# Moving copies and two tables from VectorE to ScalarE, and re-ordering TensorE's fillers, in a two-layer decoder kernel

## The chip, the cores and the metric

The kernel runs on one core of a Trainium2 chip. A core has TensorE (PE in the profile; PEld is its weight load), VectorE (DVE), ScalarE (ACT), GpSimd (POOL) and SyncE (SP), which issues the DMAs. Each engine runs its own list of instructions in order, and they wait for each other by semaphores. The metric is the device time of one execution in microseconds (us).

## The reference

The input `x` is (2, 512, 128), with a context (2, 154, 128). Six blocks are added to `x` one after the other: an attention with a window (A), a top-32 cross attention (B), an FP4-quantised feed-forward (C), a six-layer linear-attention encoder (D), a cross attention (E), and a six-layer block (F), which is more than half of the time and the place of nearly all of the change. F computes:

```python
for i in range(DEPTH):                       # DEPTH = 6
    x = attn_layer(shift_tokens(x), Wqkv[i], q_scale[i], k_scale[i], Wo[i]) + x
    x = ffn_layer(shift_tokens(x), ln_g[i], ln_b[i], W1[i], b1[i], W2[i], b2[i]) + x
# shift_tokens: the second half of the 128 channels moves by one position
# attn_layer:  qkv = x @ Wqkv, 16 heads of 64; q = l2norm(q) * qs; k = l2norm(k) * ksc
#              rotary position with a scale per channel, window 32 (each block sees itself and the one before),
#              softmax(8 * q k^T) v, then @ Wo
# ffn_layer:   xn = layernorm(x) * g + b; a, gate = split(xn @ W1 + b1)  (341 columns each)
#              (a * gelu(gate)) @ W2 + b2
```

## The kernel before

Activations stay in SBUF for the whole kernel, channels on the 128 partitions and 512 positions of a batch along the free dimension. PSUM is one tensor `ps` with eight banks of 128x512; `take` makes PE wait until the last reader of a bank is done, `read` is what that reader says. Most tiles are parts of one buffer, `big` or `fix`, so the profile's names say little and its line numbers more.

F has twelve **units**, numbered 0 to 11 here: layer 0 with batch 0, layer 0 with batch 1, layer 1 with batch 0, and so on. A unit is the attention of its layer and batch. The feed-forward of unit n runs as **hooks** inside the attention of unit n+1 (which has the other batch), so that the two chains fill each other's waits. All orders are written out by hand, one function for each engine. One unit has three parts.

- **Head**: `a_proj_pe`, with what `a_tail_pe` of the unit before has already done (pairs 0 to 2). Heads are handled as eight pairs p = 0..7. For each pair PE makes Q and K (L285, L290) in banks p % 2 and 2 + p % 2, ACT squares them (L487, L489), DVE multiplies them with the rotary tables (`a_rope_dve`, L607, L608), SP swaps neighbouring partitions by DMA (L738), and POOL adds (L705, L706). PE sums the squares (`a_ss_pe`, L331, bank 5), ACT makes the reciprocal roots in three steps (L513, L515, L516, signal `n_ready`), and PE spreads them over the partitions (`a_spread_q_pe`, `a_spread_k_pe`; L339 for pair 0, L341 for the others, from a three-part bf16 copy made by ACT and DVE). V has eight products of 512 columns (`a_v_pe`, L274), copied by ACT (L479). In the head stand the hooks of the feed-forward before: centre (L2015), variance (L2030), three pairs of products gate and up (L2038, L2040; ACT's Gelu L2105, DVE's product L2159), and `f_down_pe` (L2046), three products that end in bank Y = 7.
- **Steps** p = 0..7 (`a_steps_pe`): the mask is written into banks 0 and 1 (L372, or L367 at p = 7), which waits for DVE's last read of them; `a_scores_pe` (L384) adds the scores; DVE (`a_top_dve`) takes the maximum (L656 twice) and subtracts it (L659 twice), then multiplies Q of the next pair with its spread (L621), then sums the exponentials (L642, L649); ACT takes the exponential (L542); POOL normalises (L714, two halves). PE transposes the probabilities of step p-1 (`a_turn_pe`, L398), ACT copies them (L554), PE multiplies those of step p-2 with V (`a_values_pe`, L415), ACT copies the result (L547), PE adds pair p-3 to the output (`a_out_pe`, L425). DVE has late hooks: after step 1 it adds the feed-forward of the unit before to `x` (`f_add_dve`, L2164), after step 3 it copies `x` shifted into `xsh` for the next unit (`shift_dve`, L2133, L2134), and after step 5 of every odd unit but the last it scales the rotary tables for the next layer (`f_tab_dve`, L2171, four products). Below, "top of step p" is the group L656, L659.
- **Tail** (`a_tail_pe`): what is left of steps 6 and 7 on PE, with Q and K of pairs 0 to 2 of the next unit between.

The attention A uses the same functions without the spreads and without the feed-forward.

## Time and profile before

| | |
|---|---|
| median of 3 runs | 1751.95 us (1751.57 to 1753.41) |
| the profiled execution | 1752.89 us |
| its span, first to last instruction | 1751.1 us |
| PE busy | 1573.1 us, 90% |
| DVE, ACT, POOL busy | 1183.6, 904.8, 593.2 us (68%, 52%, 34%) |
| mean granted clock of PE | 0.961 |

Busy shares are means over blocks with different limits. A row of the timeline is a run of equal instructions: its start, its length, the line, and in brackets how long the engine had been idle before, with what ended that. The ends of matmuls are modelled, so for products back to back the distance between starts is the better measure: in F a product of 128x512 f32 (two passes) starts 0.86 us after the one before.

### The profile page before, as it was taken

The numbers are of one execution on the slowest core, as the hardware profiler recorded it, in microseconds if no ns is written. First come the engines' busy times: TensorE is split into PE (matmuls) and PEld (weight loads), VectorE is DVE, ScalarE is ACT, GpSimd is POOL, SyncE is SP. The second block draws the span as 40 slices with busy tenths as digits, with TensorE's granted clock in tenths as the row PEclk, the third lists the DMA queues.
The fourth block names the chain that finished last, engine by engine and source line by source line (L and its number), as shares of the span: only waits on it lengthen the run. The fifth ranks groups of instructions, "written<-read, shape, count | busy, mean of one in ns | idle before, by whom it ended". The sixth has DMA issues, their size and how long they took to land.

```text
span 1751.1 us, 37919 instructions
## 1 busy us (share of the span) xinstructions
PE 1573.1 (90%) x15445; PEld 855.6 (49%) x15445; DVE 1183.6 (68%) x2048; ACT 904.8 (52%) x1584; POOL 593.2 (34%) x552
## 2 busy tenths in 40 slices
PE   7887569999999998779999999999999999999996
PEld 2645336565566554223645445363545545353543
DVE  5686576656566654347778778677877867787773
ACT  2435334344533443335665656666566666666663
POOL 5362000000000000105564655445465655555561
PEclk9899779999999999879999999999999999999998
DMA  7134100000000000203041322314142231314120
GB/s 248 28 118 193 54 0 7 2 21 1 21 21 1 21 1 1 93 1 122 30 145 60 96 99 70 129 33 135 56 125 82 86 125 31 127 65 131 68 64 13
DMA packets 50668, 119.41 MB, mean 68 GB/s; under 512 B 15297, under 2 KB 20161, under 8 KB 48321
## 3 DMA queue, kind: packets, MB, share of 16 engines
q1 hardware_dynamic: 50496, 116.99, 20.3%
q8 instruction: 125, 2.05, 0.5%
q14 instruction: 47, 0.38, 0.1%
HBM read 37.52 MB, written 0.52 MB: 22 GB/s over the span
## 4 chain that ended last, share of the span: by engine, by line
PE 52%; DVE 28%; ACT 9%; issue 5%; DMA 3%; POOL 2%; SPq 1%; DVEq 0%; ACTq 0%
DVE nm L656 4%; PE ps L1583 3%; DVE nm L642 3%; PE ps L285 3%; PE ps L425 3%; PE ps L415 3%; PE ps L290 3%; PE ps L1636 3%; PE ps L274 3%; DVE big L659 2%; PE ps L1645 2%; DMA big<-big 2%; DVE big L607 2%; PE ps L1602 2%; DVE big L608 2%
## 5 line engine op out<-in xcount | busy, mean ns | idle before, releaser
L714 POOL TENSOR_TENSOR big<-big,nm 128x384 f32<-128x384 f32 x224 | 189.7, 867 | 186.5 <-DVE nm L649 186.5
L705 POOL TENSOR_TENSOR big<-big 128x512 f32<-128x512 f32 x112 | 143.3, 1280 | 310.8 <-DMA big<-big 309.8
L607 DVE TENSOR_TENSOR big<-ps,big 128x512 f32<-128x512 f32 x224 | 153.7, 686 | 87.3 <-ACT sq L487 55.8
L542 ACT ACTIVATE big<-big 128x384 f32<-128x384 f32 x224 | 109.4, 522 | 126.7 <-DVE big L659 126.6
L1427 POOL MEMSET big<- 128x512 f32 x1 | 0.5, 526 | 489.0 <-DVE x L1910 489.0
L608 DVE TENSOR_TENSOR big<-ps,big 128x512 f32<-128x512 f32 x224 | 152.5, 681 | 0.0
L415 PE MATMUL ps<-big 128*64 128x64 f32 x3584 | 130.6, 226 | 23.1 <-ACT big L554 22.9
L415 PEld LDWEIGHTS ps<-big 128*64 128x64 f32 x3584 | 116.5, 139 | 63.5 <-ACT big L554 46.6
L706 POOL TENSOR_TENSOR big<-big 128x512 f32<-128x512 f32 x112 | 144.5, 1290 | 0.0
L1870 DVE TENSOR_TENSOR big<-ps,fix 128x512 f32<-128x512 f32 x192 | 119.2, 683 | 37.3 <-PE ps L1583 36.9
L398 PE MATMUL ps<-ident,big 128*128 128x128 f32 x896 | 129.3, 283 | 15.2 <-POOL big L714 13.2
L698 POOL TENSOR_TENSOR big<-big 128x512 f32<-128x512 f32 x84 | 107.2, 1276 | 71.7 <-ACT big L534 71.6
L656 DVE TENSOR_REDUCE nm<-ps 128x4 f32<-128x384 f32 x224 | 112.3, 543 | 26.9 <-PE ps L384 24.3
L554 ACT ACTIVATE big<-ps 128x512 f32<-128x512 f32 x224 | 122.3, 594 | 9.8 <-PE ps L398 8.0
L479 ACT ACTIVATE big<-ps 128x512 f32<-128x512 f32 x112 | 66.7, 595 | 112.8 <-PE ps L274 112.8
L398 PEld LDWEIGHTS ps<-ident,big 128*128 128x128 f32 x896 | 97.8, 142 | 40.5 <-POOL big L714 27.3
L659 DVE TENSOR_TENSOR big<-ps,nm 128x384 f32<-128x384 f32 x224 | 113.5, 549 | 0.3
L642 DVE TENSOR_REDUCE nm<-big 128x8 f32<-128x768 f32 x96 | 91.5, 953 | 21.8 <-ACT big L542 20.0
L274 PE MATMUL ps<-big,xsh 128*128 128x512 f32 x192 | 104.7, 628 | 0.0
L384 PE MATMUL ps<-big 64*64 64x96 f32 (+1 forms) x3584 | 97.3, 244 | 5.5 <-DVE big L627 2.2
L285 PE MATMUL ps<-xsh,big 128*128 128x512 f32 x192 | 100.6, 606 | 0.2 <-DVE big L608 0.2
L425 PE MATMUL ps<-fix,big 128*128 128x512 f32 x192 | 99.6, 600 | 0.7 <-ACT fix L547 0.7
(301 smaller groups left out, 2930.9 us busy)
## 6 DMA issues: line engine op xcount, KB each, us to landing
big<-big SPq DMA_DIRECT2D x224, 256.0 KB, 2.4
big<-big SPq DMA_DIRECT2D x112, 128.0 KB, 2.4
big<-in_F_w SPq DMA_DIRECT2D x6, 1536.0 KB, 7.0
big<-in_zero SPq DMA_DIRECT2D x8, 1088.0 KB, 12.5
big<-big SPq DMA_DIRECT2D x84, 64.0 KB, 2.0
big<-in_D_w SPq DMA_DIRECT2D x12, 256.0 KB, 3.0
big<-in_F_wo SPq DMA_DIRECT2D x6, 512.0 KB, 4.3
big<-in_F_w SPq DMA_DIRECT2D x6, 341.0 KB, 3.0
```

The lines of the kernel that those rows point to most:

```text
L274: pe.matmul(ps[:, kv, :], src_of(key, b)[:, 128 * t:128 * t + 128], Wqkv[:, 2, 512 * hf:512 * hf + 512], start=True, stop=True).then_inc(* ...
L285: pe.matmul(ps[:, kq, :], Wqkv[:, 0, 128 * p:128 * p + 128], src_of(key, b), start=True, stop=True).then_inc(*full[kq].mark((key, b, "q", p)))
L398: last = pe.transpose(ps[:, 4 + h, 128 * j:128 * j + 128], P[:, 2 * (p % 2) + h, at0:at0 + 128], ident[:, :])
L415: last = pe.matmul(ps[64 * h:64 * h + 64, 6, 64 * m:64 * m + 64], vv[:, m // 2, 128 * p + 64 * h:128 * p + 64 * h + 64], PT[:, 2 * (p % 2) ...
L425: last = pe.matmul(ps[:, Y, :], Wo[:, p, :], ot(key, p), start=p == 0, stop=p == NP - 1)
L607: dve.tensor_tensor(tmp[:, i, w, :], ps[:, k, :], tb[:, 2 * w, :], ALU.mult).then_inc(*part.mark((key, b, p, 0)))
L608: dve.tensor_tensor(sinp[:, i, T * w:T * w + T], ps[:, k, :], tb[:, 2 * w + 1, :], ALU.mult).then_inc(*part.mark((key, b, p, 1)))
L642: dve.tensor_reduce(nm[:, i, 8:16].rearrange("p (h j) -> p h j", h=2), P[:, g:g + 2, :].rearrange("p h (j k) -> p h j k", j=4)[:, :, :, 0: ...
L656: dve.tensor_reduce(nm[:, i, 4 * h:4 * h + 4], s4(h), AX, ALU.max).then_inc(*topped.mark((key, b, p, h)))
L659: dve.tensor_tensor(shft[:, 2 * (p % 2) + h, :].rearrange("p (j k) -> p j k", j=4), s4(h), nm[:, i, 4 * h:4 * h + 4].unsqueeze(2).to_broad ...
L706: pool.tensor_tensor(KT[:, p, :], tmp[:, i, 1, :], swp[:, i, T:2 * T], ALU.add).then_inc(*k_added.mark((key, b, p)))
L714: pool.tensor_tensor(v, v, nm[:, p % 3, 16 + 4 * h:20 + 4 * h].unsqueeze(2).to_broadcast([128, 4, KW]), ALU.mult)\
```

## The change

Five things are changed.

1. The shifted copy of `x` into `xsh` for the next unit and the scaling of the rotary tables go from DVE to ACT: `f_move_act` after step 3, `f_tab_act` in two halves after steps 4 and 5 of odd units. The tables of layer 0 are still made by DVE.
2. DVE adds the feed-forward to `x` before step 0 instead of after step 1. `f_down_pe` is cut: its first two products stand behind the spreads of pair 0, its third behind the scores of step 0.
3. The third `up` product of the feed-forward goes to bank 2 instead of bank 7.
4. On PE, V 5 stands before the spreads of pair 0, and in steps 1 to 6 the spreads stand between the mask and the scores instead of behind the scores.
5. In the tail, Q 0 of the next unit stands before the values of step 6 and K 0 behind them; Q 1 and K 1 stand before the output product of pair 6.

The transposes of the probabilities stay as they are.

```diff
@@ a_qk_pe is split @@
-        def a_qk_pe(pe, key, b, p):
-            kq, kk = p % 2, 2 + p % 2
+        def a_q_pe(pe, key, b, p):
...
+        def a_k_pe(pe, key, b, p):
...
+        def a_qk_pe(pe, key, b, p):
+            a_q_pe(pe, key, b, p)
+            a_k_pe(pe, key, b, p)
@@ a_proj_pe @@
                 a_ss_pe(pe, key, b, NP // 2 - 1)
-                a_v_pe(pe, key, b, 4)
+            a_v_pe(pe, key, b, 4)
+            a_v_pe(pe, key, b, 5)
+            if l2:
+                a_spread_q_pe(pe, key, b, 0)
+                a_spread_k_pe(pe, key, b, 0)
                 if "down" in hooks:
                     hooks["down"]()
-                a_spread_q_pe(pe, key, b, 0)
-                a_spread_k_pe(pe, key, b, 0)
-            else:
-                a_v_pe(pe, key, b, 4)
-            a_v_pe(pe, key, b, 5)
@@ a_steps_pe @@
                 a_mask_pe(pe, key, b, p, l2)
+                if l2 and p >= 2 and p + 2 < NP:
+                    a_spread_k_pe(pe, key, b, p + 2)
+                if l2 and 0 < p < NP - 1:
+                    a_spread_q_pe(pe, key, b, p + 1)
                 a_scores_pe(pe, key, b, p, l2)
-                if l2 and p + 1 < NP:
-                    a_spread_q_pe(pe, key, b, p + 1)
                 if l2 and p == 0:
+                    a_spread_q_pe(pe, key, b, 1)
                     a_spread_k_pe(pe, key, b, 1)
+                if p in late:
+                    late[p]()
                 if p < 2:
                     a_v_pe(pe, key, b, NT + 2 + p)
-                if l2 and p + 2 < NP:
-                    a_spread_k_pe(pe, key, b, p + 2)
-                if p in late:
-                    late[p]()
+                    if l2:
+                        a_spread_k_pe(pe, key, b, p + 2)
@@ a_tail_pe @@
+            if nxt:
+                a_q_pe(pe, *nxt, 0)
             a_values_pe(pe, key, b, NP - 2)
+            if nxt:
+                a_k_pe(pe, *nxt, 0)
             a_out_pe(pe, key, b, NP - 3)
-            if nxt:
-                a_qk_pe(pe, *nxt, 0)
             a_turn_pe(pe, key, b, NP - 1)
-            a_out_pe(pe, key, b, NP - 2)
             if nxt:
                 a_qk_pe(pe, *nxt, 1)
...
+            a_out_pe(pe, key, b, NP - 2)
             a_values_pe(pe, key, b, NP - 1)
@@ a_rope_dve, attn_dve @@
+            if l2 and n == -3 and key[1] > 0:
+                dve.wait_ge(*tab_made.at((key[1], 1)))
...
                     a_parts_dve(dve, key, b)
+                if "down" in early:
+                    early["down"]()
@@ f_up_pe, f_down_pe, f_pe_hooks @@
+        UP = (7, 7, 2)
...
-            take(pe, 7)
-            pe.matmul(ps[0:m, 7, :], W1[:, c0:c0 + m], fxn, start=True, stop=True).then_inc(*full[7].mark(("F", l, b, "up", i)))
+            take(pe, UP[i])
+            pe.matmul(ps[0:m, UP[i], :], W1[:, c0:c0 + m], fxn, start=True, stop=True).then_inc(*full[UP[i]].mark(("F", l, b, "up", i)))
...
-                     "up": lambda: f_up_pe(pe, *u, 2), "down": lambda: f_down_pe(pe, *u)}, {})
+                     "up": lambda: f_up_pe(pe, *u, 2), "down": lambda: f_down_pe(pe, *u, (0, 1))}, {0: lambda: f_down_pe(pe, *u, (2,))})
@@ new functions of ACT, and their hooks @@
+        def f_move_act(act, l, b):
+            act.wait_ge(*x_new.at(("Ff", l, b)))
+            step(act, act_step, act.activation(xsh[0:64, b, :], x[0:64, cols(b)], ACT.Copy))
+            act.activation(xsh[64:128, b, 1:T], x[64:128, T * b:T * b + T - 1], ACT.Copy).then_inc(moved, 1)
+
+        def f_tab_act(act, l, i):
+            act.wait_ge(scl_in, 16 * (l + 1))
+            act.wait_ge(*k_part.at((("F", l - 1), B - 1, NP - 1, 1)))
+            for j in (2 * i, 2 * i + 1):
+                ins = act.activation(tab[:, j, :], tab0[:, j, :], ACT.Copy, scale=scl[:, i:i + 1])
+            ins.then_inc(*tab_made.mark((l, i)))
...
+            l, late = key[1], {3: lambda: f_move_act(act, *u)}
+            if b == B - 1 and l + 1 < LAYERS:
+                late[4], late[5] = lambda: f_tab_act(act, l + 1, 0), lambda: f_tab_act(act, l + 1, 1)
@@ f_dve_hooks @@
-            def move():
-                dve.wait_ge(*x_new.at(("Ff", *u)))
-                shift_dve(dve, u[1], (moved, 1))
...
-                early = {4: lambda: f_scale_dve(dve, *u), 6: lambda: f_mul_dve(dve, *u, 0), 7: multiply}
-                late[1], late[3] = lambda: f_add_dve(dve, *u), move
+                early = {4: lambda: f_scale_dve(dve, *u), 6: lambda: f_mul_dve(dve, *u, 0), 7: multiply,
+                         "down": lambda: f_add_dve(dve, *u)}
...
-            if b == B - 1 and l + 1 < LAYERS:
-                late[5] = lambda: f_tab_dve(dve, l + 1)
```

How the order moves. On PE, from the last sum of squares in the head to the spread of K of pair 2, in unit 1, before (L331 sum of squares, L274 V, L2046 down, L339 and L341 spreads, L372 mask, L384 scores):

```order
L331 MATMUL ps<-big 32x512 x4
L274 MATMUL ps<-big,xsh 128x512
L2046 MATMUL ps<-fix,big 128x512 x3
L339 MATMUL ps<-rs,big 128x512 x2
L274 MATMUL ps<-big,xsh 128x512
L372 MATMUL ps<-band,identb 64x384 x4
L384 MATMUL ps<-big 64x64 x2
L384 MATMUL ps<-big 64x96 x14
L341 MATMUL ps<-xn,big 128x512 x2
L274 MATMUL ps<-big,xsh 128x512
L341 MATMUL ps<-xn,big 128x512
```

And in the changed kernel, where the same are L336, L274, L2064, L344, L346, L377 and L389:

```order
L336 MATMUL ps<-big 32x512 x4
L274 MATMUL ps<-big,xsh 128x512 x2
L344 MATMUL ps<-rs,big 128x512 x2
L2064 MATMUL ps<-fix,big 128x512 x2
L377 MATMUL ps<-band,identb 64x384 x4
L389 MATMUL ps<-big 64x64 x2
L389 MATMUL ps<-big 64x96 x14
L346 MATMUL ps<-xn,big 128x512 x2
L2064 MATMUL ps<-fix,big 128x512
L274 MATMUL ps<-big,xsh 128x512
L346 MATMUL ps<-xn,big 128x512
```

V 5 has moved ahead of the spreads, and one of the three down products now stands behind the scores of step 0.

On DVE, from the last of the three parts to the add of the feed-forward, in the same unit, before (L636 last part of the three, L656 and L659 top, L621 Q, L642 and L649 sum, L2164 the add):

```order
L636 SCALAR_TENSOR_TENSOR xn<-xn,eps,sq 128x512
L656 TENSOR_REDUCE nm<-ps 128x4 x2
L659 TENSOR_TENSOR big<-ps,nm 128x384 x2
L621 TENSOR_TENSOR big<-big,ps 128x512
L642 TENSOR_REDUCE nm<-big 128x8
L649 RECIPROCAL nm<-nm 128x8
L656 TENSOR_REDUCE nm<-ps 128x4 x2
L659 TENSOR_TENSOR big<-ps,nm 128x384 x2
L621 TENSOR_TENSOR big<-big,ps 128x512
L642 TENSOR_REDUCE nm<-big 128x8
L649 RECIPROCAL nm<-nm 128x8
L2164 SCALAR_TENSOR_TENSOR x<-ps,big,x 128x512
```

And changed (L648, L668, L671, L633, L654, L661, and L2199 for the add):

```order
L648 SCALAR_TENSOR_TENSOR xn<-xn,eps,sq 128x512
L2199 SCALAR_TENSOR_TENSOR x<-ps,big,x 128x512
L668 TENSOR_REDUCE nm<-ps 128x4 x2
L671 TENSOR_TENSOR big<-ps,nm 128x384 x2
L633 TENSOR_TENSOR big<-big,ps 128x512
L654 TENSOR_REDUCE nm<-big 128x8
L661 RECIPROCAL nm<-nm 128x8
L668 TENSOR_REDUCE nm<-ps 128x4 x2
```

The add now stands ahead of the top of step 0.

On PE, the end of step 7 and the tail of unit 1, before (L415 values, L398 transposes, L425 output, L285 and L290 Q and K of the next unit):

```order
L415 MATMUL ps<-big 64x64 x16
L398 MATMUL ps<-ident,big 128x128 x8
L425 MATMUL ps<-fix,big 128x512
L415 MATMUL ps<-big 64x64 x16
L425 MATMUL ps<-fix,big 128x512
L285 MATMUL ps<-xsh,big 128x512
L290 MATMUL ps<-xsh,big 128x512
L398 MATMUL ps<-ident,big 128x128 x8
L425 MATMUL ps<-fix,big 128x512
```

And changed (L420, L403, L430, L284, L292):

```order
L420 MATMUL ps<-big 64x64 x16
L403 MATMUL ps<-ident,big 128x128 x8
L430 MATMUL ps<-fix,big 128x512
L284 MATMUL ps<-xsh,big 128x512
L420 MATMUL ps<-big 64x64 x16
L292 MATMUL ps<-xsh,big 128x512
L430 MATMUL ps<-fix,big 128x512
L403 MATMUL ps<-ident,big 128x128 x8
L284 MATMUL ps<-xsh,big 128x512
```

One Q product now stands ahead of the values of step 6, and its K product behind them.

## Rows read from the trace of the kernel before

**Rows 1.** Waits of PE in F: us in total, times, longest.

```profile
PE ps L415 <- ACT big L554: 18.3, 39, 1.1
PE ps L372 <- DVE big L659: 9.8, 22, 0.5
PE ps L2040 <- DVEq L136: 6.1, 6, 1.4
```

**Rows 2.** Instructions of L689: ns min/median/max, first and last start in us.

```profile
L689 DVE TENSOR_TENSOR x<-x,ps x14: 686/689/689, 90.2 to 1723.8; 128x512 f32<-128x512 f32 x14
```

**Rows 3.** Timeline, PE, unit 7, V 4 to step 1: start us, us, instruction.

```profile
1364.40 1.13 PE L274 MATMUL ps<-big,xsh 128*128 128x512 f32 x2
1365.36 2.74 PE L2046 MATMUL ps<-fix,big 128*128 128x512 f32 x6
1368.03 1.13 PE L339 MATMUL ps<-rs,big 32*128 32x512 f32 x4
...
1370.70 0.89 PE L384 MATMUL ps<-big 64*64 64x64 f32 x32 [0.20 <-DVE big L627]
...
1371.84 1.13 PE L274 MATMUL ps<-big,xsh 128*128 128x512 f32 x2
...
1373.72 0.36 PE L372 MATMUL ps<-band,identb 64*64 64x384 bf16 x4 [0.43 <-DVE big L659]
```

**Rows 4.** Timeline, ACT, unit 7, the reciprocal roots.

```profile
1364.73 0.69 ACT L513 ACTIVATE rs<-ps,eps 128x512 f32<-128x512 f32 x1
...
1366.29 0.72 ACT L516 ACTIVATE rs<-rs,eps 128x512 f32<-128x512 f32 x1
1367.04 0.63 ACT L518 ACTIVATE xn<-rs 128x512 bf16<-128x512 f32 x1
```

**Rows 5.** Timeline, DVE, unit 7, steps 0 to 2.

```profile
1371.62 1.02 DVE L656 TENSOR_REDUCE nm<-ps 128x4 f32<-128x384 f32 x2 [0.41 <-PE ps L384]
...
1375.17 0.95 DVE L642 TENSOR_REDUCE nm<-big 128x8 f32<-128x768 f32 x1 [1.01 <-ACT big L542]
...
1379.87 0.70 DVE L2164 SCALAR_TENSOR_TENSOR x<-ps,big,x 128x512 f32<-128x512 f32 x1
```

**Rows 6.** Timeline, PE, unit 6, head to tail.

```profile
1286.12 1.09 PE L2040 MATMUL ps<-xc,big 128*85 128x512 f32 x2 [0.98 <-DVEq L136]
...
1301.06 1.44 PE L398 MATMUL ps<-ident,big 128*128 128x128 f32 x8 [0.52 <-POOL big L714]
...
1304.79 1.31 PE L398 MATMUL ps<-ident,big 128*128 128x128 f32 x8
1306.56 0.36 PE L372 MATMUL ps<-band,identb 64*64 64x384 bf16 x4 [0.46 <-DVE big L659]
...
1317.27 1.15 PE L415 MATMUL ps<-big 128*64 128x64 f32 x32 [0.20 <-ACT big L554]
...
1324.37 0.49 PE L367 MATMUL ps<-bandw,identb 128*128 128x384 bf16 x2
...
1329.78 1.15 PE L415 MATMUL ps<-big 128*64 128x64 f32 x32 [1.14 <-ACT big L554]
```

**Rows 7.** Timeline, PE, unit 5 (with tables), steps 7 and tail.

```profile
1246.59 0.48 PE L367 MATMUL ps<-bandw,identb 128*128 128x384 bf16 x2 [0.82 <-DVE big L659]
...
1248.56 1.15 PE L415 MATMUL ps<-big 128*64 128x64 f32 x32 [0.58 <-ACT big L554]
...
1252.31 1.15 PE L415 MATMUL ps<-big 128*64 128x64 f32 x32 [0.67 <-ACT big L554]
```

**Rows 8.** Waits of ACT in F: us in total, times, longest.

```profile
ACT big L542 <- DVE big L659: 94.6, 66, 4.0
```

**Rows 9.** Windows: PE, PEld, DVE, ACT, POOL busy (instructions), PE clock, DMA, GB/s.

```profile
820.00:824.00 4.00, 1.44 (x6) 0.30 (x2) 3.54 (x6) 3.27 (x6) 0.81 (x2) 1.00 0.48 161
824.00:832.00 8.00, 7.89 (x47) 2.96 (x47) 6.99 (x9) 2.00 (x4) 6.99 (x5) 0.57 0.50 141
1246.00:1250.00 4.00, 2.82 (x69) 2.23 (x70) 3.82 (x8) 2.69 (x6) 1.55 (x2) 1.00 0.01 4
```

More of the change, by code:

```diff
@@ L281, in a_qk_pe @@
             if p < 2:
-                take(pe, kq)
+                take(pe, p)
             else:
                 pe.wait_ge(*q_part.at((key, b, p - 2, 1)))
-            pe.matmul(ps[:, kq, :], Wqkv[:, 0, 128 * p:128 * p + 128], src_of(key, b), start=True, stop=True).then_inc(*full[kq].mark((key, b, "q", p)))
+            pe.matmul(ps[:, p % 2, :], Wqkv[:, 0, 128 * p:128 * p + 128], src_of(key, b), start=True, stop=True).then_inc(*full[p % 2].mark((key, b, "q", p)))
+        def a_k_pe(pe, key, b, p):
+            kk = 2 + p % 2
             if p < 2:
@@ L1998, in build @@
         f_const, scl_in, ff_in_ = raw("f_const"), raw("scl_in"), raw("ff_in_")
-        tab_made = sg("tab_made")
+        tab_made, tab_first = sg("tab_made"), sg("tab_first")
         F_FF = 5 * 16
@@ L2038, in f_up_pe, with f_down_pe @@
             pe.matmul(ps[0:m, 6, :], W1[:, DI + c0:DI + c0 + m], fxn, start=True, stop=True).then_inc(*full[6].mark(("F", l, b, "gate", i)))
-            take(pe, 7)
-            pe.matmul(ps[0:m, 7, :], W1[:, c0:c0 + m], fxn, start=True, stop=True).then_inc(*full[7].mark(("F", l, b, "up", i)))
-        def f_down_pe(pe, l, b):
-            take(pe, Y)
-            for i, (c0, m) in enumerate(DIC):
+            take(pe, UP[i])
+            pe.matmul(ps[0:m, UP[i], :], W1[:, c0:c0 + m], fxn, start=True, stop=True).then_inc(*full[UP[i]].mark(("F", l, b, "up", i)))
+        def f_down_pe(pe, l, b, parts):
+            for i in parts:
+                if i == 0:
+                    take(pe, Y)
+                m = DIC[i][1]
                 pe.wait_ge(*f_mul.at((l, b, i)))
                 last = pe.matmul(ps[:, Y, :], W2[0:m, i, :], fh[0:m, i, :], start=i == 0, stop=i == 2)
-            last.then_inc(*full[Y].mark(("F", l, b, "f2")))
+            if i == 2:
+                last.then_inc(*full[Y].mark(("F", l, b, "f2")))
         def f_before(l, b):
@@ L2070, in f_pe @@
                 f_up_pe(pe, *u, i)
-            f_down_pe(pe, *u)
+            f_down_pe(pe, *u, range(3))
         def f_square_act(act, l, b):
@@ L2119, in f_act_hooks @@
             return ({3: lambda: f_square_act(act, *u), 4: lambda: f_root_act(act, *u), 5: lambda: f_xn_act(act, *u), 6: lambda: f_gelu_act(act, *u, 0),
-                     7: lambda: f_gelu_act(act, *u, 1), "up": last}, {})
+                     7: lambda: f_gelu_act(act, *u, 1), "up": last}, late)
         def f_act(act):
@@ L2156, in f_mul_dve @@
             m = DIC[i][1]
-            dve.wait_ge(*full[7].at(("F", l, b, "up", i)))
+            dve.wait_ge(*full[UP[i]].at(("F", l, b, "up", i)))
             dve.wait_ge(*gg.at((l, b, i)))
-            dve.scalar_tensor_tensor(fh[0:m, i, :], ps[0:m, 7, :], b1[0:m, i:i + 1], fg[i % 2][0:m, :], ALU.add, ALU.mult).then_inc(*f_mul.mark((l, b, i)))
-            read(dve, 7, f_mul, (l, b, i))
+            dve.scalar_tensor_tensor(fh[0:m, i, :], ps[0:m, UP[i], :], b1[0:m, i:i + 1], fg[i % 2][0:m, :], ALU.add, ALU.mult).then_inc(*f_mul.mark((l, b, i)))
+            read(dve, UP[i], f_mul, (l, b, i))
         def f_add_dve(dve, l, b):
@@ L2171, in f_tab_dve @@
                 ins = dve.tensor_scalar(tab[:, j, :], tab0[:, j, :], scl[:, j // 2:j // 2 + 1], None, ALU.mult)
-            ins.then_inc(*tab_made.mark(l))
-            dve.wait_ge(*tab_made.at(l))
+            ins.then_inc(*tab_first.mark(l))
+            dve.wait_ge(*tab_first.at(l))
         def f_dve_hooks(dve, key, b):
@@ L2247, in f_sp @@
                 if l + 1 < LAYERS:
-                    sp.wait_ge(*tab_made.at(l))
+                    sp.wait_ge(*(tab_made.at((l, 1)) if l else tab_first.at(0)))
                     f_w_sp(sp, l + 1)
```

## The prediction

> **What bounds the kernel now.** I read the busy shares first, then who waits for whom on PE in F, then the timelines of PE, DVE and ACT over two units. F's units follow each other in 77.2 us: the last add of a unit first starts at 875.0 us in F and last at 1723.8, eleven units on [rows 2]. PE sets that length. Over the 27 us of a head it has at most one gap above 0.3 us, and its four steps 3 to 6 take 17.8 us (1306.56 to 1324.37 [rows 6]), nearly all of it work. What it loses stands in short waits that come back at the same places in every unit: for ACT's copies of the transposes ahead of the values (18.3 us in 39 waits), for DVE's subtraction ahead of the mask (9.8 us), and for bank 7 ahead of the third `up` product (6.1 us in six heads, those of unit 5 and the even units from 2 on) [rows 1]. So the question is what each new order does to these waits. DVE is next: where a hook stands in its steps it, and not PE, sets the pace.
>
> **Head to step 0.** Take unit 7, whose head has no wait for bank 7. V 4 starts at 1364.40 [rows 3], 0.86 us of work. V 5 now comes next, but it needs bank 5, which L513 reads until 1365.42 [rows 4]: it starts at 1365.5, not at 1365.3, and takes PE to 1366.5. The spreads of pair 0 wait for `n_ready`, which is L516's end, 1367.01 [rows 4]; so PE idles 0.6 us where it had none, and the spreads start at 1367.1 instead of 1368.03 [rows 3]. They take 1.06. Two down products (0.86 each, from 2.74 for three: 2 x 0.86 + 1.02 [rows 3]) end at about 1369.95, and the scores follow 0.36 after the mask, at 1370.3 instead of 1370.70: **-0.4**. In even units the wait of 0.98 for bank 7 goes too [rows 6], since bank 2 was last read by the rotary products of pair 6, long done. There L513 had waited for the sums of squares behind it; it moves forward until it meets the end of the table load, so nearly all of it is kept: **-1.0** more.
>
> **Step 0.** This is where the change costs. DVE's add now stands ahead of the top of step 0, and the add waits for the third down product. From the scores' start: scores and spreads 1.14 (1370.70 to 1371.84), product 1.02, 0.1 to hand over [rows 3], so the add starts at 1370.3 + 2.26 = 1372.55. An add of this form holds DVE 0.8 (0.70 and its signal [rows 5]). The top of step 0 starts at 1373.35 and not at 1371.62 [rows 5], and the mask of step 1, which waits for that top, moves from 1373.72 [rows 3] by the same: **+1.75** in odd units, **+0.75** in even ones. PE has nothing for the time: behind the product it has V 6 and one spread, as before.
>
> **Steps 1 to 3.** Some of it comes back. (a) The sum of step 0 waited 1.01 us for ACT's exponential [rows 5], which ACT took up late behind V 6 and the spread's copy; these now come before the top is done. The sum starts 0.95 earlier against the mask, and so do POOL and the transposes, ahead of which PE waited 0.52 and which took 1.44 where those a step later took 1.31 and nothing but POOL's second half held them [rows 6]: **-0.8**. (b) The add no longer stands in DVE's way after step 1 (1379.87 [rows 5]): that was the mask's wait of 0.46 before step 3 and, with it, slower scores and values in step 3 [rows 6]. Of some 0.9 in all I take **-0.65**, the rest staying as a wait.
>
> **Steps 3 to 6.** DVE's copies (1.35 us) go: the wait of 0.20 ahead of values at step 5 [rows 6] goes with them, **-0.2**. PE works without gaps there, so no more can come. The spreads in front of the scores delay scores by 0.3 and so top, exponential and copies; the values of step p need the copies of the transposes of p-2, which by the trace were ready about as much ahead of them. I take 0, bounded by -0.2 and by +0.3 in each of six steps (+1.8 a unit). In odd units with tables the four DVE products go, which made PE wait 0.82 before the mask of step 7 and 0.58 behind it, against 0.67 instead of 1.14 in the tail [rows 6, 7]: 0.82 + 0.58 - 0.47 = **-0.93** in five units.
>
> **What ACT takes over.** Two copies per unit, four table copies in five units. The trace has no ACT copy of 64 rows; the nearest are 0.63 us (the bf16 copy of the reciprocal roots) and 0.72 with an operand per partition [rows 4], so 0.63 to 0.72 each, 1.3 for a pair. ACT waits for DVE's subtraction 94.6 us over F in 66 waits, 1.4 on average [rows 8]. Behind `f_move_act` stands the spread's copy and then the exponential of the next step, which waits for just that subtraction: the pair fits with 0.1 us to spare. So 0, bounded above by the pair in full, 1.3 x 11 moves + 2.6 x 5 tables = 27 us. ACT's only wait that could be new is for `scl`; its DMA is issued in step 1 and lands some 6.5 us later, before step 4.
>
> **The tail.** Values of step 6 wait 1.14 us for ACT's copies in plain units and 0.67 after tables [rows 6, 7]. Q 0 (0.86) now fills that: the values start where they did, and all that follows is one product shorter: **-0.86**. Q 0 needs bank 0, free when the top of step 7 is done, 1.2 us before, and `xsh`, copied by ACT three steps earlier. ACT's squares can begin earlier, so the rotary part gets a start; PE had no wait there, so 0. Q 1 and K 1 before the output of pair 6 swap work that both was ready: 0.
>
> **The sum.** Odd units with tables: +1.75 - 0.8 - 0.65 - 0.2 - 0.93 - 0.86 = -1.7. Even units: +0.75 - 0.8 - 0.65 - 0.2 - 0.86 = -1.75. Five of each: -17.25. Unit 5 has a wait for bank 7 too, 0.65: -0.65. Unit 0 has no feed-forward and gets the tail only: -0.86. Unit 11 has neither tables nor a next unit: +1.75 - 0.8 - 0.65 - 0.2 = +0.1. In A the waits of the tail are elsewhere: 0. Total -18.7. The profiled execution took 1752.89 us (span 1751.1); that gives 1734.2, and on the median of 1751.95 it gives **1733 us**, 1.1% less.
>
> **Rivals.**
> *A, the late product costs nothing.* If the top of step 0 is not delayed, or if steps 1 to 3 give all of it back, +1.75 and +0.75 fall away: 6 x 1.75 + 5 x 0.75 = 14, so 1719. For it: DVE has 4 us a unit less to do in the steps than before. Against: PE, not DVE, sets steps 3 to 6, so DVE's slack buys nothing there, and DVE is in order.
> *B, ACT's new work comes onto the path.* The copies of the transposes stand behind it, and PE already waits for these more than for anything [rows 1]. If half of the 27 us shows, the time is 1747; that is still faster, just so.
> *C, the clock falls in each unit, and the kernel is slower.* [...] The order of now never brings this on in units 1 to 10: even 1246 to 1250, with PE idle 1.2 of 4 us, stayed at 1.00 [rows 9]. The new order gathers 0.6 us ahead of the spreads and, from there 5 us on, a wait ahead of the mask of step 1: PE reaches it at 1373.7 and the mask comes at 1375.45, 1.7 us, more than any wait F has now outside units 0 and 11. [...]
> [...]
>
> **How the numbers follow.** My forecast 0.64, A 0.16, B 0.12, C 0.08. A measurement of this kernel tells a difference of about 0.2%, 3.5 us. The forecast's own range is 1724 to 1741, from the ends of the ACT and scores terms. A pulls to 1715 and B to 1747: 1713 to 1747 leaves out most of C and little else. Faster: 0.62 + 0.16 + 0.10 = 0.88; within 0.2%: 0.05; slower: 0.07.
>
> **What would show it.** In the new profile of a middle unit: (1) no wait at the third `up`; (2) a wait of 0.5 to 0.7 us ahead of the spreads of pair 0; (3) the add directly behind the third down product, and a wait of 1.2 to 1.8 us ahead of the mask of step 1, the largest of the unit; (4) values of step 6 with a wait of 0.3 or less and Q 0 in front; (5) steps 3 to 6 in some 17 us instead of 17.8, with waits ahead of the values below 0.2; (6) clock 1.00 in units 1 to 10; (7) a unit of 75.5 us instead of 77.2. Waits of 0.5 and more for L564 (ACT's copies) would speak for B; a granted clock below 1 in the middle of F, for C; no wait at (3), for A. I am wrong if steps 3 to 6 take less than 16.5 us, since then PE was not what set them.

## The result, and the profile after

| | before | changed |
|---|---|---|
| median, timed on the same chip | 1752.68 us | 1780.79 us (1778.61 to 1785.29) |
| ratio, 95% interval | | 1.0165 (1.0148 to 1.0183) |
| profiled execution, span | 1752.89, 1751.1 us | 1778.61, 1776.8 us |
| PE busy | 1573.1 us | 1605.6 us |
| mean granted clock | 0.961 | 0.948 |

It is 1.6% slower; the forecast was 1733, in 1713 to 1747. In the changed kernel L377 and L372 are the mask, L389 the scores, L344 (pair 0) and L346 the spreads, L420 the values, L403 the transposes, L430 the output, L284 and L292 Q and K, L2064 down, L2056 `up`, L2029 the centre. Engine rows of its page (busy us, share, instructions):

```profile
PE 1605.6 (90%) x15445; PEld 863.2 (49%) x15445; DVE 1182.4 (67%) x2006; ACT 927.4 (52%) x1626; POOL 590.0 (33%) x552
```

PE executes the same 15445 instructions, and yet is busy 32.5 us longer: it ran more of them slowly. Then who PE waits for in F (line, releaser: us in total, times, longest):

```profile
PE ps L377 <- DVE big L671: 20.4, 11, 1.9
PE ps L2056 <- DVEq L136: 7.5, 7, 1.7
PE ps L420 <- ACT big L564: 6.0, 22, 1.0
PE ps L344 <- ACT rs L526: 4.6, 11, 0.4
PE ps L2029 <- DVE xsh L2169: 2.1, 10, 0.3
```

Against [rows 1] the waits for ACT's copies fell from 18.3 to 6.0 us, those for DVE's subtraction rose from 9.8 to 20.4 and lie in one place, and a wait for `xsh` is new. The wait for bank 7 is gone from the third `up`, but it has come back at the second, and is longer there: 7.5 us in seven heads, where it was 6.1 in six. The timeline of PE in unit 7, which answers to [rows 3]:

```profile
1382.91 2.24 PE L274 MATMUL ps<-big,xsh 128*128 128x512 f32 x4
1385.58 1.13 PE L344 MATMUL ps<-rs,big 32*128 32x512 f32 x4 [0.42 <-ACT rs L526]
...
1388.55 0.36 PE L377 MATMUL ps<-band,identb 64*64 64x384 bf16 x4
...
1393.97 0.36 PE L377 MATMUL ps<-band,identb 64*64 64x384 bf16 x4 [1.85 <-DVE big L671]
...
1395.61 1.13 PE L274 MATMUL ps<-big,xsh 128*128 128x512 f32 x2
...
1396.98 1.20 PE L403 MATMUL ps<-ident,big 128*128 128x128 f32 x8
...
1400.04 1.15 PE L420 MATMUL ps<-big 128*64 128x64 f32 x32 [0.42 <-ACT big L564]
```

The mask waits 1.85 us, for DVE's subtraction, which stands behind the add (DVE in unit 7: the add, the maximum, the subtraction):

```profile
1390.98 0.75 DVE L2199 SCALAR_TENSOR_TENSOR x<-ps,big,x 128x512 f32<-128x512 f32 x1 [1.95 <-PE ps L2064]
1391.87 1.02 DVE L668 TENSOR_REDUCE nm<-ps 128x4 f32<-128x384 f32 x2
1392.81 1.01 DVE L671 TENSOR_TENSOR big<-ps,nm 128x384 f32<-128x384 f32 x2
```

The same stretch of unit 6 begins alike and goes on otherwise:

```profile
1313.42 0.36 PE L377 MATMUL ps<-band,identb 64*64 64x384 bf16 x4 [1.85 <-DVE big L671]
...
1315.05 2.08 PE L274 MATMUL ps<-big,xsh 128*128 128x512 f32 x2
...
1317.59 1.97 PE L403 MATMUL ps<-ident,big 128*128 128x128 f32 x8
...
1320.49 1.53 PE L389 MATMUL ps<-big 64*64 64x64 f32 x32
```

The same products take 2.08 instead of 1.13 us, and 1.97 instead of 1.20. The windows of the two stretches (unit 6, then unit 7; columns as in [rows 9]) say why:

```profile
1308.00:1321.00 13.00, 11.00 (x112) 5.50 (x115) 8.59 (x16) 6.17 (x12) 5.76 (x6) 0.77 0.31 76
1389.00:1402.00 13.00, 10.45 (x158) 5.84 (x149) 9.98 (x21) 6.68 (x13) 7.15 (x8) 1.00 0.41 113
```

The granted clock was 0.77 in the first, a mix of 1.00 up to 1315.0 and 0.50 from there on, and 1.00 in the second. A fall of the clock stands behind the wait in nine of the eleven units (not in 1 and 7); in units 2, 3, 5, 6 and 10 the granted clock over steps 0 to 3 is 0.84, in 4, 8, 9 and 11 it is 0.91. Over the span, 1776.8 x (1 - 0.948) = 92 us of full-speed work are lost, against 1751.1 x (1 - 0.961) = 68 before.

Where the time went, from the starts of the masks in units 1 to 10 (sums in us; the forecast is my terms put into the same parts, good to some 0.5 each):

| part of a unit | before | changed | difference | forecast |
|---|---|---|---|---|
| step 0 | 35.7 | 55.0 | +19.3 | +19.0 |
| steps 1 to 3 | 140.4 | 146.5 | +6.2 | -14.5 |
| steps 4 to 6 | 133.7 | 130.8 | -2.9 | -6.1 |
| mask of step 7 to the next unit's first | 466.9 | 467.3 | +0.4 | -16.3 |
| sum | 776.7 | 799.6 | +22.9 | -17.9 |

Another 3.3 us lie ahead of unit 1, 2.8 of them in unit 0 (79.15 instead of 76.34). So three parts are off, and the one that I called the cost is not among them.

### The profile page after: what moved, and what is told of

The parts are those of the page before. It is cut to its first block, busy times and chain, and to the rows that moved or that the text cites. A ratio compares the mean times of both kernels' runs of the same rounds, so it can differ in the third digit from the quotient of the medians.

```text
span 1776.8 us, 37924 instructions
## 1 busy us (share of the span) xinstructions
PE 1605.6 (90%) x15445; PEld 863.2 (49%) x15445; DVE 1182.4 (67%) x2006; ACT 927.4 (52%) x1626; POOL 590.0 (33%) x552
## 4 chain that ended last, share of the span: by engine, by line
PE 60%; DVE 19%; ACT 11%; issue 4%; DMA 2%; POOL 2%; SPq 0%; DVEq 0%; ACTq 0%; POOLq 0%
PE ps L420 5%; PE ps L403 5%; PE ps L430 5%; PE ps L389 4%; PE ps L1597 3%; PE ps L292 3%; PE ps L1650 3%; DVE big L619 3%; DVE big L620 3%; DVE nm L668 2%; PE ps L1659 2%; DMA big<-big 2%; PE ps L274 2%; PE ps L284 2%; PE ps L1616 2%
## 5 line engine op out<-in xcount | busy, mean ns | idle before, releaser
L728 POOL TENSOR_TENSOR big<-big,nm 128x384 f32<-128x384 f32 x224 | 185.0, 847 | 182.4 <-DVE nm L661 182.4
L668 DVE TENSOR_REDUCE nm<-ps 128x4 f32<-128x384 f32 x224 | 114.2, 551 | 52.0 <-PE ps L389 48.1
L403 PE MATMUL ps<-ident,big 128*128 128x128 f32 x896 | 131.5, 291 | 8.3 <-POOL big L728 7.3
L420 PE MATMUL ps<-big 128*64 128x64 f32 x3584 | 129.2, 225 | 10.6 <-ACT big L564 10.1
L420 PEld LDWEIGHTS ps<-big 128*64 128x64 f32 x3584 | 115.1, 138 | 44.4 <-ACT big L564 26.7
L403 PEld LDWEIGHTS ps<-ident,big 128*128 128x128 f32 x896 | 102.8, 147 | 31.2 <-POOL big L728 13.3
L671 DVE TENSOR_TENSOR big<-ps,nm 128x384 f32<-128x384 f32 x224 | 113.2, 546 | 0.0
L274 PE MATMUL ps<-big,xsh 128*128 128x512 f32 x192 | 110.3, 660 | 0.0
L654 DVE TENSOR_REDUCE nm<-big 128x8 f32<-128x768 f32 x96 | 91.5, 953 | 26.9 <-ACT big L552 25.2
L389 PE MATMUL ps<-big 64*64 64x96 f32 (+1 forms) x3584 | 102.9, 252 | 1.5 <-DVE big L639 1.5
L284 PE MATMUL ps<-xsh,big 128*128 128x512 f32 x192 | 101.7, 611 | 2.1 <-DVE big L620 2.1
L292 PE MATMUL ps<-xsh,big 128*128 128x512 f32 x192 | 100.5, 605 | 0.8
```

Source lines behind the costliest of these rows:

```text
L274: pe.matmul(ps[:, kv, :], src_of(key, b)[:, 128 * t:128 * t + 128], Wqkv[:, 2, 512 * hf:512 * hf + 512], start=True, stop=True).then_inc(* ...
L284: pe.matmul(ps[:, p % 2, :], Wqkv[:, 0, 128 * p:128 * p + 128], src_of(key, b), start=True, stop=True).then_inc(*full[p % 2].mark((key, b, ...
L292: pe.matmul(ps[:, kk, :], Wqkv[:, 1, 128 * p:128 * p + 128], src_of(key, b), start=True, stop=True).then_inc(*full[kk].mark((key, b, "k", p)))
L389: last = pe.matmul(ps[64 * c_:64 * c_ + 64, h, KW * j + k0:KW * j + KW], Q[rows, p, 64 * m:64 * m + 64], KT[rows, p, 64 * m - WIN + k0:64 ...
L403: last = pe.transpose(ps[:, 4 + h, 128 * j:128 * j + 128], P[:, 2 * (p % 2) + h, at0:at0 + 128], ident[:, :])
L420: last = pe.matmul(ps[64 * h:64 * h + 64, 6, 64 * m:64 * m + 64], vv[:, m // 2, 128 * p + 64 * h:128 * p + 64 * h + 64], PT[:, 2 * (p % 2) ...
```

## The experiments

In step lengths below, a step is the time from one mask to the next. All kernels compute the whole reference. They were timed on three chips; each ratio is to the kernel before on the same chip, whose medians there are 1752.6 to 1753.8. Where two runs come from different chips, a difference of their medians is good to a few us.

### The late add, and the clock behind its wait

`x1_add_late` is the changed kernel with DVE's add behind step 1 again:

```diff
-                early = {4: ..., 6: ..., 7: multiply, "down": lambda: f_add_dve(dve, *u)}
+                early = {4: ..., 6: ..., 7: multiply}
+                late[1] = lambda: f_add_dve(dve, *u)
```

> The changed kernel with one edit: DVE adds the feed-forward to x after step 1 again, as before the change; the three down products stay where the change put them. Theory 1 (the add ahead of the top of step 0 makes the mask of step 1 wait 1.85 us, and that wait brings the clock down in 9 of 11 units): the interval from the mask of step 0 to that of step 1 goes from 5.42 to about 3.7 us, no fall of the granted clock in the middle of F; 11 x 1.7 for the wait and 9 x 2.2 for the clock, less some 0.5 a unit that the add costs at its old place: about 1748 us. Theory 2 (it is the spreads between mask and scores, 0.16 us in every step): the time stays within 5 us of the changed kernel's 1781. Theory 3 (the heads lose it, since the new tail makes the shifted copy meet POOL's adds): also within 5 us of 1781.

Measured: 1760.91 us, ratio to before 1.0041 (1.0025 to 1.0058); 20 us come back. Step 0 takes 3.50 instead of 5.42, but step 1 takes 5.48 instead of 4.14: PE waits before the transposes.

```profile
1381.29 1.44 PE L403 MATMUL ps<-ident,big 128*128 128x128 f32 x8 [1.24 <-POOL big L728]
```

Its cause is on ACT, which in this unit had DVE's subtraction (done by 1376.7) to work on, but stood at V 6, whose product came later; the exponential follows the second of these rows, at 1378.2:

```profile
1376.97 0.60 ACT L489 ACTIVATE big<-ps 128x512 f32<-128x512 f32 x1 [1.29 <-PE ps L274]
1377.69 0.60 ACT L544 ACTIVATE big<-ps 128x512 f32<-128x512 f32 x1
```

So step (a) of the forecast was real, but it was bought by the early add: without that, V 6 and the spread's copy stand in the exponential's way as before, and V 6 comes later still, since the third down product now stands ahead of it (step 1 takes 5.48 where it took 4.98 before the change). The clock still fell in five units, here behind the wait of 1.24. With that wait and those falls the time is 13 us above the 1748 that theory 1 gave.

`x2_fill` leaves the order of the changed kernel and puts two products that nobody reads into PE's wait before the mask of step 1 (into bank 4, which is free there):

```diff
+                    if l2 and p == 0 and (key, b) != F_UNITS[0]:
+                        pe.wait_ge(*v_ready.at((key, b, 4)))
+                        for _ in range(2):
+                            pe.matmul(ps[:, 4, :], src_of(key, b)[:, 0:128], Wqkv[:, 2, 0:512], start=True, stop=True)
```

> The changed kernel with two extra products of 128x512 f32 into bank 4, which nobody reads, in PE's wait ahead of the mask of step 1 in units 1 to 11 (1.72 us of work in a wait of 1.85). Every other wait stays. Theory 1: the mask comes at the same distance from the scores as in the changed kernel, but the granted clock stays at 1.00 in the middle of F, and what the falls cost goes, 9 x 2.2 = 20 us: about 1761 us. If the falls have another cause, or cost nothing since the time is lost in waits anyway: 1781, with the falls still there. If PE's wait is not real slack: 1781 + up to 19.

Measured: 1754.56 us, 1.0006 (0.9991 to 1.0022): 26.2 us less than the changed kernel, by added work. Unit 6, PE, then the window of that stretch:

```profile
1299.55 1.98 PE L454 MATMUL ps<-big,xsh 128*128 128x512 f32 x4
1301.48 0.36 PE L377 MATMUL ps<-band,identb 64*64 64x384 bf16 x4
```

```profile
1296.00:1309.00 13.00, 12.43 (x169) 6.79 (x169) 9.96 (x20) 6.25 (x12) 6.66 (x7) 1.00 0.37 89
```

The mask comes as late as before (step 0 5.43), yet the clock stays at 1.00, in all of units 1 to 10. Steps 1 to 3 take 13.1 in every unit, where the changed kernel had 13.1 to 15.7. They give 15.4 us; unit 2's step 0 and unit 11's steps 1 to 3, where falls stood too, give 1.7 more. The heads give 7.8, but not by the falls as far as can be seen: they are 0.9 and 1.2 us shorter also behind units 1 and 7, which had no fall in the changed kernel. What shortened them was not followed. This settles rival C: nothing but PE's idleness was taken away, and the falls went. They had cost some 17 us by the steps; the 26.2 between the two kernels is an upper bound. And the 1.00 behind the filled wait shows that products which nobody reads will do.

`x14_add_early` asks the same of the best order found by then (`x10_shift_act`, below), with the add ahead of step 0 again:

```diff
-                early = {4: ..., 6: ..., 7: multiply}
-                late[1] = lambda: f_add_dve(dve, *u)
+                early = {4: ..., 6: ..., 7: multiply, "down": lambda: f_add_dve(dve, *u)}
```

> The best kernel so far (1725 us) with the add ahead of the top of step 0 again, that is with the part under suspicion alone put back. Theory 1: the mask of step 1 waits 1.85 us more in 11 units, step 1 to 3 give some 0.9 back, and the clock falls in most of units 1 to 11, 2.2 us each: 1725 + 10 + 20 = 1755 us, with a granted clock below that of the kernel it comes from. If the clock falls only together with the other parts of the change: 1735 us.

Measured: 1750.12 us, 0.9985 (0.9975 to 0.9995), against 1725.25: the early add costs 24.9 us there by the medians and 29 by the ratios (two chips), and I wrote 30. The clock falls in eight of the eleven units. Its unit 4, with a fall, and its unit 6, without (columns as in [rows 9]):

```profile
1134.40:1150.30 15.90, 13.90 (x169) 7.94 (x168) 10.57 (x21) 6.65 (x13) 7.90 (x8) 0.79 0.32 77
1290.40:1306.30 15.90, 13.01 (x209) 7.49 (x207) 12.68 (x25) 8.74 (x19) 8.24 (x9) 1.00 0.32 78
```

A unit is 74.57 with the late add, 76.07 with the early one at full clock, and 76.5 to 78.3 with a fall. So the wait alone costs 1.5 us a unit, 16 of the 25, and the falls 0.5 to 2.2 each, 11.6 in units 1 to 10. Unit 0 gives 2.6 back.

### The spreads ahead of the scores

`x3_spread_behind` is the changed kernel with the spreads behind the scores in steps 1 to 6; `x4_both` has that and the late add of `x1_add_late`.

```diff
                 a_mask_pe(pe, key, b, p, l2)
+                a_scores_pe(pe, key, b, p, l2)
                 if l2 and p >= 2 and p + 2 < NP:
                     a_spread_k_pe(pe, key, b, p + 2)
                 if l2 and 0 < p < NP - 1:
                     a_spread_q_pe(pe, key, b, p + 1)
-                a_scores_pe(pe, key, b, p, l2)
```

> The changed kernel with one edit: in steps 1 to 6 the spreads stand behind the scores again. Theory 2 (mask, spread, scores costs PE 0.16 us more a step than mask, scores, spread): steps 4 and 5 go from 4.39 to 4.23 us, 12 units x 6 steps x 0.16 = 11.5 us: about 1769 us. Theory 1 alone: the wait ahead of the mask of step 1 and the falls of the clock stay, and steps 4 and 5 stay at 4.39 us because ACT or DVE set them: 1779 to 1783.

> The changed kernel with both edits: the add after step 1, and the spreads behind the scores. If theories 1 and 2 both hold and add up: 1748 - 11.5 = 1737 us, below the kernel before (1752). If the head's losses (theory 3, a wait of up to 1.7 us for bank 7 at the second up product) are what is left: no better than 1745.

Measured: 1769.99 us, 1.0108 (1.0087 to 1.0128), and 1750.52, 0.9982 (0.9964 to 1.0000); the second is again 13 us above its forecast, with the wait ahead of the transposes (1.38 here) and six falls. Between the kernels that differ only in the order of the spreads lie 10.8 us with the early add and 10.4 with the late one. Part of it is a cost on PE itself. Step 6 of the changed kernel in unit 6:

```profile
1337.87 0.36 PE L377 MATMUL ps<-band,identb 64*64 64x384 bf16 x4
1338.16 0.38 PE L346 MATMUL ps<-xn,big 32*128 32x512 bf16 x1
1338.47 0.89 PE L389 MATMUL ps<-big 64*64 64x64 f32 x32
1339.29 1.15 PE L420 MATMUL ps<-big 128*64 128x64 f32 x32
```

And of `x3_spread_behind`:

```profile
1330.93 0.36 PE L377 MATMUL ps<-band,identb 64*64 64x384 bf16 x4
1331.12 0.83 PE L389 MATMUL ps<-big 64*64 64x64 f32 x32
1331.88 0.39 PE L346 MATMUL ps<-xn,big 32*128 32x512 bf16 x1
1332.19 1.15 PE L420 MATMUL ps<-big 128*64 128x64 f32 x32
```

From mask to values it is 1339.29 - 1337.87 = 1.42 against 1332.19 - 1330.93 = 1.26, with no wait in either: mask to spread takes 0.29 where mask to scores took 0.19, spread to scores 0.31 and scores to values 0.82, where they took 0.76 and 0.31. That is +0.16 in each of steps 4, 5 and 6 (4.39, 4.39, 4.30 instead of 4.23, 4.23, 4.14), or 5 us over ten units. Another 2.2 lie in unit 0 (77.0 instead of 79.2). The rest is in heads and falls, which differ from unit to unit, and is not shown to come from the order.

### ACT's copies alone, the tail alone, and the shifted copy

`x6_act_only` is the kernel before with part 1 of the change (ACT's copies and tables), `x5_tail_only` the kernel before with part 5:

```diff
 @@ x6_act_only, f_dve_hooks @@
-                late[1], late[3] = lambda: f_add_dve(dve, *u), move
+                late[1] = lambda: f_add_dve(dve, *u)
-                late[5] = lambda: f_tab_dve(dve, l + 1)
 @@ x5_tail_only, a_tail_pe @@
+            if nxt:
+                a_q_pe(pe, *nxt, 0)
             a_values_pe(pe, key, b, NP - 2)
+            if nxt:
+                a_k_pe(pe, *nxt, 0)
             a_out_pe(pe, key, b, NP - 3)
-            if nxt:
-                a_qk_pe(pe, *nxt, 0)
             a_turn_pe(pe, key, b, NP - 1)
-            a_out_pe(pe, key, b, NP - 2)
             if nxt:
                 a_qk_pe(pe, *nxt, 1)
 ...
+            a_out_pe(pe, key, b, NP - 2)
             a_values_pe(pe, key, b, NP - 1)
```

> The kernel before with the copies after step 3 and the tables on ACT, all else as before. The prediction's terms: nothing on ACT's side, -0.2 us a unit for the copies, -0.93 in five units for the tables: 11 x 0.2 + 5 x 0.93 = 7 us, about 1746 us. The rival (ACT's new work comes onto the path): waits of PE for ACT's copies at steps 4 to 6 grow, 1752 or more.

> The kernel before with the new tail alone (Q 0 ahead of the values of step 6, K 0 behind them, Q 1 and K 1 ahead of the output of pair 6). The prediction's term: the wait of 0.67 or 1.14 us before the values of step 6 falls to 0.2, 11 x 0.86 = 9.5 us: about 1743 us. Theory 3 (an earlier start of the rotary part makes the shifted copies on DVE meet POOL's adds, 1.4 us each instead of 0.42, and the swaps come late, so that the heads give it back as waits for bank 7): the wait in the tail goes, the heads grow by about as much, and the time is within 3 us of 1752.

Measured: 1746.40 us, 0.9944 (0.9928 to 0.9960), and 1766.37, 1.0047 (1.0024 to 1.0069). ACT's part does what its terms said: step 5 goes from 4.51 to 4.23, step 6 of table units from 5.12 to 4.14, and the new copies are short and delay nothing on PE (unit 6, ACT; the exponential still waits for DVE behind them):

```profile
1308.47 0.62 ACT L2128 ACTIVATE xsh<-x 64x512 f32<-64x512 f32 x1
1309.12 0.63 ACT L2129 ACTIVATE xsh<-x 64x511 f32<-64x511 f32 x1
...
1310.63 0.99 ACT L548 ACTIVATE big<-big 128x384 f32<-128x384 f32 x2 [0.26 <-DVE big L667]
```

The tail, forecast at -0.86 a unit, makes the kernel slower. Its heads take from 44.91 us, which is 45.77 - 0.86, up to 47.43 behind the five plain units, where the kernel before has 45.77 in three, 45.84 and 46.66. Its twelve times lie in two groups, 1750.5 to 1758.3 (four) and 1764.5 to 1769.0 (eight), the lower one at a granted clock of 0.959 to 0.962 and the upper one at 0.954 to 0.959; the profiled one is of the lower group. What eats the gain is seen in the chain of work of the changed kernel, head of unit 8 (start us, us, what):

```profile
1435.98 0.70 DVE x L703
...
1436.81 1.39 DVE xsh L2168
...
1446.97 4.36 DMA big<-big
...
1451.39 1.27 POOL big L719
1452.67 1.23 POOL big L720
...
1453.92 0.69 DVE big L619
...
1456.87 0.76 DVE fix L2194
...
1457.73 1.13 PE ps L2056 x2
```

The chain leaves PE at the end of the unit and comes back 22 us later: the last add to `x`, the shifted copy on DVE, the rotary products, their swap by DMA, POOL's adds, the next products, the feed-forward's product, and the second `up`, which waited 1.73 for bank 7. So a delay at DVE's copy comes out at PE. This copy is the one at a unit's end, of `x` with the attention added, which the feed-forward reads; it is not the one that part 1 of the change moved. And it is delayed: DVE and POOL in the changed kernel (the first two blocks), then DVE in the kernel before.

```profile
1436.81 1.38 DVE L2168 COPY xsh<-x 64x512 f32<-64x512 f32 x1
1438.23 1.39 DVE L2169 COPY xsh<-x 64x511 f32<-64x511 f32 x1
```

```profile
1436.65 1.27 POOL L719 TENSOR_TENSOR big<-big 128x512 f32<-128x512 f32 x1
1437.87 1.46 POOL L720 TENSOR_TENSOR big<-big 128x512 f32<-128x512 f32 x1
```

```profile
1341.88 0.42 DVE L2133 COPY xsh<-x 64x512 f32<-64x512 f32 x1
```

Alone the copy takes 0.42 us. Started 0.16 after one of POOL's adds it takes 1.38, which ends 0.3 after that add; the next one ends 0.3 after POOL's second add. The new tail starts the rotary part earlier, and so brings POOL's adds to where the copies are. The profile of `x5_tail_only` bears it out head by head: of its five behind plain units, the one of 44.91 us has both copies at 0.42, the two of 45.03 and 45.74 have the second at 1.38, and the two of 46.03 and 47.43 have both at 1.39 to 1.47. So 1.38 is what was left of the add (1.1) and 0.3 more.

`x11_tail_shift` tests it: `x5_tail_only` with the shifted copy at a unit's end on ACT. `x12_shift_only` is the kernel before with that alone.

```diff
+        def f_shift_act(act, l, b):
+            act.wait_ge(*x_new.at((("F", l), b)))
+            step(act, act_step, act.activation(xsh[0:64, b, :], x[0:64, cols(b)], ACT.Copy))
+            act.activation(xsh[64:128, b, 1:T], x[64:128, T * b:T * b + T - 1], ACT.Copy).then_inc(*shifted.mark((l, b)))
 @@ it is called first thing in a_proj_act; DVE's hooks @@
-            late[NP + 2] = lambda: f_shift_dve(dve, l, b)
```

> The kernel before with the new tail and with the shifted copy at the end of a unit on ACT; all else as before. The new tail alone gave times in two groups, 1750 to 1758 and 1764 to 1769. Theory 3 (the tail's earlier start makes DVE's two copies meet POOL's adds, and the heads lose what the tail gains): with the copies on ACT all heads are alike, from the mask of step 7 to the next of step 0 in some 44.9 us in plain units, and the time is one group, 9.5 us below 1753 from the tail and 6 us more from the waits for bank 7: 1738 to 1742. If the losses come from the swaps by DMA and not from the copies: two groups again, the upper above 1755.

> The kernel before with only the shifted copy at the end of a unit on ACT. With the old tail DVE's copies took 0.42 us each, so there is nothing in them to gain but the waits for bank 7 in six heads, 6.1 us: 1747 us at best by theory 3, and 1753 if those waits come from the swaps.

Measured: 1742.93 us, 0.9943 (0.9930 to 0.9957), in one group of 1741.61 to 1744.09; and 1748.91, 0.9980 (0.9970 to 0.9990). By the ratios the copy alone is worth 3.5 us, the tail with it another 6.5, and the tail without it costs 8. Heads behind plain units are now 44.91 in every one: the forecast -0.86, as worked out. Behind units with tables, which these two kernels still make on DVE, there is no gain: 45.70 to 46.94 with the new tail against 46.34 to 46.53 without, with waits for bank 7 of 0.8 to 1.1 in four of five. `x12_shift_only` has none of those waits above 0.2.

### A version that beats both

`x9_exp_first` is `x4_both` with ACT's exponential of step 0 ahead of V 6 and the spread's copy, which is what the early add had given; `x10_shift_act` adds the shifted copy on ACT; `x13_exp_first_twice` does in step 1 what `x9_exp_first` does in step 0.

```diff
+                if l2 and p == 0:        # x13_exp_first_twice: p < 2
+                    a_exp_act(act, key, b, p, l2)
                 if p < 2:
 ...
-                a_exp_act(act, key, b, p, l2)
+                if not (l2 and p == 0):  # x13_exp_first_twice: p < 2
+                    a_exp_act(act, key, b, p, l2)
```

> The changed kernel with the add after step 1, the spreads behind the scores, and on ACT the exponential of step 0 ahead of the copies of V 6 and of the spread for pair 2. In the run with the first two edits alone, the third down product holds back V 6, and ACT, in order, held back the exponential for both: PE waited 1.4 us ahead of the transposes of step 1, and the clock fell there in six of eleven units. If that is the cause: step 1 takes some 4.5 us instead of 5.48, the granted clock stays at 1.00 in units 1 to 10, and the time is 11 x 1 + 6 x 1 = 17 us below the 1750.5 of that run, about 1734 us. If POOL or the heads hold it: no better than 1746.

> The same, with the shifted copy at the end of a unit on ACT too (two copies of 0.62 us ahead of ACT's squares of pair 3). Theory 3: DVE's two copies took 1.39 us each in the heads since they met POOL's adds; without them the rotary products of pair 2 start 2.8 us earlier, the wait for bank 7 at the second up product goes (up to 1.7 us a unit), and the time is 5 to 10 us below the kernel it is compared with. If the swaps by DMA hold the heads: within 2 us of it.

> The best kernel so far (the changed one with the add after step 1, the spreads behind the scores, ACT's exponential first in step 0, the shifted copy on ACT; 1725 us) with the exponential first in step 1 as well. DVE's sum of step 1 waited 0.99 us for it, and PE 0.46 ahead of the mask of step 3 in 11 units. If ACT's order is the cause: 0.5 us a unit, 1719 to 1720 us. If POOL or the add hold the mask: 1725.

Measured: 1736.07 us, 0.9882 (0.9862 to 0.9901); 1725.25, 0.9819 (0.9797 to 0.9840); and 1713.20, 0.9780 (0.9763 to 0.9797), the fastest here. The steps go from 3.50, 5.48, 4.12, 4.94 to 3.50, 4.81, 3.92, 4.94 and then 3.50, 4.88, 3.59, 4.49. In `x9_exp_first` heads run from 44.86 to 49.49, the longest with a fall of the clock behind a wait of 1.69 for bank 7; in `x10_shift_act`, with the copy on ACT, from 44.80 to 45.35. The last was forecast at 1719 to 1720: its units are 0.7 us shorter, 7.6 in ten of them, somewhat more than the forecast 0.5; 4.5 more lie ahead of F's first mask, where the two kernels do the same, and belong to the runs. What PE still waits for in F in the last:

```profile
PE ps L403 <- POOL big L733: 7.8, 11, 0.7
PE ps L420 <- ACT big L566: 6.0, 22, 1.1
```

No wait for the mask is left among the first, and no fall in units 1 to 10.

## Why the prediction was wrong

What held: the wait at the mask of step 1 (check 3: 1.85 us, forecast 1.7, and the largest of every unit); a wait ahead of the spreads (2), though of 0.42 and not of 0.5 to 0.7; 0.18 ahead of the values of step 6 (4); no wait at the third `up` (1); the earlier exponential, (a): step 1 took 4.14 instead of 4.98, -0.84 for -0.8; ACT's new work at no cost, and DVE's copies and tables worth some 7 us. Checks 5 to 7 failed: steps 3 to 6 take 17.65 us where the clock did not fall, the clock fell, and a unit is 77.4 to 81.8 us. What failed in the working, in the order of size:

1. **Rival C came true, and I gave it 0.08.** The failing step is the evidence that I weighed it by. I had one stretch of each kind [rows 9]: PE idle 2.6 of 4 us, with a clock of 0.57 over the 8 us behind, and idle 1.2 of 4 us at 1.00. The 1.7 us to come is nearer to the 1.2, and I took that distance for a chance. The 1.2 was not even one wait: it is two, of 0.82 and 0.58 [rows 7], cut at the window's edge. And eleven units are eleven tries. Nine fell; `x2_fill` shows that PE's idleness is the cause, and `x14_add_early` that the same wait does it with nearly everything else changed (8 of 11). The price per fall was too high in its turn. From 0.57 over 8 us I took 8 x 0.43 = 3.4 us of full-speed work, eleven times 37, which makes 1770; in steps 1 to 3 a fall cost 1.1 to 2.6, 15.4 in the ten units and some 17 in all. So that 1770 came nearest to 1780.79 is in part luck: the falls made 17 of its 37 us, and the items below made up for the rest. The windows of 1 us show 3.4 us of full-speed work lost in units 2, 3, 5, 6 and 10 and 1.7 in 4, 8, 9 and 11, so part of it is hidden by the waits that PE would have had.
2. **The tail's -0.86, and the head.** The failing step is the reason given for its last term: "ACT's squares can begin earlier, so the rotary part gets a start; PE had no wait there, so 0". I counted a head start as harmless. It moved POOL's adds onto DVE's copies, and the way from there back to PE had no slack. In place of -16.3 the heads gave +0.4 (and -7.4 in `x2_fill`). That also took the terms for bank 7, five times -1.0 and -0.65 for unit 5: the third `up` no longer waits, but the second waits up to 1.73. With the copies on ACT the same heads take 448.9 us (`x10_shift_act`), 18.0 less than before: the gain was there, and was covered.
3. **The order of mask, spreads and scores, taken at 0.** I bounded it by what a later score would make others wait. Its cost was on PE itself: 0.16 a step with no wait at all, 5 us in steps 4 to 6, and 2 in unit 0 (`x3_spread_behind`); the whole kernels differ by 10 to 11, of which the rest was not traced. The upper bound, +0.3 a step, held it; the value I took did not.
4. **Steps 2 and 3, (b), -0.65.** Step 3 fell from 4.94 to 4.57, but step 2 rose from 4.13 to 4.40, also with the spreads behind the scores, at a wait of 0.42 for ACT's copies ahead of the values: what step 1 had gained reached PE before those copies were ready. That reading is argued from the row at 1400.04; no run took ACT's copies away. -0.10 in place of -0.65 makes 5.5 us.
5. **Unit 0, -0.86.** It became 2.8 longer; its step 0 takes 5.95 instead of 4.31. The term left out that part 4 of the change bears on unit 0 too. Before, V 5 stood between the spreads of pair 0 and the mask; now it stands ahead of the spreads, unit 0 has no down products to take its place, and PE waits ahead of the scores for DVE's product of K with its spread (before, then changed):

```profile
825.73 2.08 PE L274 MATMUL ps<-big,xsh 128*128 128x512 f32 x2
```

```profile
829.79 1.56 PE L389 MATMUL ps<-big 64*64 64x64 f32 x32 [1.01 <-DVE big L639]
```

   Every kernel here with V 5 ahead of the spreads has 5.9 to 6.9 in that step, those without it 3.9 to 4.3. The other 1.2 us are 0.16 to 0.37 in each of steps 3 to 6, gone with the spreads behind the scores (`x3_spread_behind`), and 0.3 in the head.

`x2_fill` has the rest of the change without the falls: 1754.6, no change. So items 2 to 5 alone ate the forecast gain. Of the 26 us that the changed kernel lies above it, the falls made some 17, and the heads 7.8 in a way that was not followed. A fell with the 1.85, B with `x6_act_only`.

Still open: why `x5_tail_only` has two groups of times. With the copy on ACT they are gone, so the collision has a part in it; but only a run of the lower group was profiled, and whether the collisions are more frequent in the upper one, whether the DMA swap behind them (4.36 us in the chain above) is longer, or whether its lower granted clock means a fall or two is not shown. Open too is what kept units 1 and 7 at full clock with the same wait, and what makes a head lose it: the heads of the changed kernel wait up to 1.73 for bank 7, and the clock falls in none of them.
